# Splitting the feed-forward's normalised input into two f16 parts: on GpSimd before the transposes, instead of on ScalarE and VectorE after them

## The reference, cut to what matters

```
x = L0_attn_x                                  # (32, 256, 128) float32
x = x + 0.5 * ffn(layernorm(x))                # no gamma or beta here
x = x + attention(layernorm(x))                # 16 heads, softmax, projections, a layernorm of its own
x = x + 0.5 * ffn(layernorm(x))

def ffn(x):                                    # k0, k1, k2 are booleans: weights +1 or -1
    h = concatenate([x, -x], axis=-1)
    h = s0 * (h @ sign(k0)); h = relu(h) * 2   # 128 -> 512
    h = s1 * (h @ sign(k1)); h = relu(h) * 2   # 512 -> 512
    return s2 * (h @ sign(k2))                 # 512 -> 128
```

## Time and profile before

| | before |
|---|---|
| time, median of 3 runs | 853.59 us (852.42 to 855.54) |
| the profiled execution's own time | 853.7 us |
| its span, first to last instruction | 851.9 us |
| mean granted clock of TensorE | 0.967 |
| busy: PE, DVE, ACT, POOL | 721.5, 643.5, 513.3, 375.6 us |
| four f32 transposes of one feed-forward input (L554), 32 times | 22.2 us busy |
| its high part on ScalarE and its rest on VectorE (L1008) | 592 ns and 688 ns each |

### The profile page before, as it was taken

The page is one execution under the profiler, slowest core; times in us unless marked ns, Lnnn a source line. Parts: engine busy times, 40 slices in busy tenths (PEclk is TensorE's granted clock), DMA queues, the critical chain, the costliest instruction groups (busy, mean ns, idle before and its releaser), DMA issues. The chain is left out here.

```text
span 851.9 us, 18411 instructions
## 1 busy us (share of the span) xinstructions
PE 721.5 (85%) x7258; PEld 325.4 (38%) x7258; DVE 643.5 (76%) x1228; ACT 513.3 (60%) x739; POOL 375.6 (44%) x663
## 2 busy tenths in 40 slices
PE   6768688899998988899998888899998987977666
PEld 2433234444443434444443334344443333332333
DVE  6558778878787888878787888878787887767343
ACT  3326566766666666766666666666666666656532
POOL 4522453536355353536355453536445453435240
PEclk9989899999999999999999999999999999989797
DMA  3101010101101010101101010100101010100000
GB/s 65 38 19 45 14 45 14 58 15 40 33 4 56 15 57 15 58 14 39 33 2 58 14 58 15 57 15 32 40 3 57 14 58 3 45 15 2 15 13 12
DMA packets 29508, 25.62 MB, mean 30 GB/s; under 512 B 4336, under 2 KB 29424, under 8 KB 29424
## 3 DMA queue, kind: packets, MB, share of 16 engines
q1 hardware_dynamic: 28992, 24.07, 9.1%
q10 hardware_dynamic: 432, 0.39, 0.1%
HBM read 5.05 MB, written 4.19 MB: 11 GB/s over the span
## 5 line engine op out<-in xcount | busy, mean ns | idle before, releaser
L1055 DVE TENSOR_REDUCE row_max<-ps_s 128x4 f32<-128x1024 f32 x256 | 312.4, 1220 | 89.8 <-PE ps_s L645 89.5
L830 ACT ACTIVATE probs<-ps_t,score_scale 128x1024 f32<-128x1024 f32 x256 | 283.9, 1109 | 122.8 <-PE ps_t L658 121.3
L798 ACT ACTIVATE ffn_hi<-ps_z 128x512 f16<-128x512 f32 x288 | 168.9, 592 | 139.0 <-PE ps_z L571 76.2
L1005 DVE SCALAR_TENSOR_TENSOR ffn_lo<-ps_z,ffn_hi 128x512 f16<-128x512 f32 x256 | 174.5, 686 | 74.8 <-ACT ffn_hi L798 71.9
L570 PE MATMUL ps_z<-ffn_hi,w 128*128 128x512 f16 x512 | 196.4, 384 | 5.9 <-DVE ffn_lo L1005 5.9
L571 PE MATMUL ps_z<-ffn_lo,w 128*128 128x512 f16 x512 | 194.9, 381 | 0.0
L698 PE MATMUL ps_c<-probs,v_cols 128*32 128x256 f32 x2048 | 139.6, 391 | 0.0
L645 PE MATMUL ps_s<-k_rows,q_rows 32*128 32x256 f16 x1024 | 102.4, 278 | 39.0 <-DVE row_max L1055 31.0
L658 PE MATMUL ps_t<-q_rows,k_rows 32*128 32x256 f16 x1024 | 102.2, 278 | 4.5 <-ACT probs L830 4.5
L471 POOL TENSOR_TENSOR max_scaled<-row_max,max_unit 128x16 f32<-128x16 f32 x64 | 14.2, 222 | 176.1 <-DVE row_max L1055 176.1
L570 PEld LDWEIGHTS ps_z<-ffn_hi,w 128*128 128x128 f16 x512 | 49.9, 98 | 88.4 <-issue 24.0
(11 more groups left out here) (119 smaller groups left out, 965.0 us busy)
## 6 DMA issues: line engine op xcount, KB each, us to landing
x<-L_attn_x SPq DMA_DIRECT2D x16, 256.0 KB, 2.7
q_rows<-q_hi SPq DMA_DIRECT2D x32, 128.0 KB, 2.1
y<-x SPq DMA_DIRECT2D x16, 256.0 KB, 2.1
k_rows<-k_hi SPq DMA_DIRECT2D x30, 128.0 KB, 2.1
q_rows<-q_lo SPq DMA_DIRECT2D x16, 128.0 KB, 2.1
q_rows<-no_max SPq DMA_DIRECT2D x16, 128.0 KB, 2.1
k_rows<-k_lo SPq DMA_DIRECT2D x15, 128.0 KB, 2.1
q_rows<-max_rows SPq DMA_DIRECT2D x64, 8.0 KB
```

The source lines that it names most:

```text
L798: a_.activation(ffn_hi[:, use, :], ps_z[use % 2][:], ACT.Relu if use else ACT.Copy, scale=1.0 if use else XN_SCALE).then_inc(z_hi, 1)
L830: a_.activation(probs[grp % 2][:, j:j + 2, :], ps_t[:], ACT.Exp, scale=score_scale[:, 0:1]).then_inc(s_exp, 1)
L1005: v.scalar_tensor_tensor(out=ffn_lo[:, use, :], in0=ps_z[use % 2][:], scalar=0.0, in1=ffn_hi[:, use, :], op0=ALU.max, op1=ALU.subtract).th ...
L1055: v.tensor_reduce(row_max[hb % 2][:].rearrange("p (a l) e -> p l a e", a=2)[:, j:j + 2, :, g % 2], ps_s[:].rearrange("p l (a k) -> p l a k ...
```

## The change

GpSimd's `ffn_norm` no longer calls `normalize`. The scale of 256 goes into the power: variance plus eps is multiplied by 256 to the power -2 in the same operation (now a `tensor_scalar`). The product is then made twice, once in f32 (`ffn_xn`) and once rounded to f16 (`ffn_xh`), and a third operation subtracts the two and gives the rest in f16 (`ffn_xl`). The last one waits for both. TensorE transposes the two parts with eight f16 transposes into the same bank, read as f16. ScalarE copies the whole bank, 128 x 1024 f16, into `ffn_x` in one operation, and VectorE's part in it (L1008) is gone. The first layer waits for ScalarE's copy on a semaphore of its own, `z_in`; `z_free` counts nine for each feed-forward. The buffers `ffn_hi` and `ffn_lo` lose their number 0 and are renumbered, and SyncE's waits count by nine.

```diff
@@ ffn_norm (GpSimd)
-                normalize(ffn_xn[:], src[:], ffn_mv, ffn_xc, ffn_ve, ffn_rs, TT, f_rs, 2 * f, f_xn)
+                g.tensor_scalar(ffn_ve[:], ffn_mv[:, :, 1], EPS, XN_SCALE ** -2, ALU.add, ALU.mult).then_inc(f_rs, 1)
+                g.tensor_tensor(ffn_xc[:], src[:], ffn_mv[:, :, 0:1].broadcast_to(shape), ALU.subtract).then_inc(f_split, 1)
+                pool.wait_ge(f_rs, 2 * f + 1)
+                g.tensor_tensor(ffn_rs[:], ffn_ve[:], minus_half[:, 0:TT], ALU.pow).then_inc(f_rs, 1)
+                pool.wait_ge(f_rs, 2 * f + 2)
+                pool.wait_ge(f_split, 3 * f + 1)
+                g.tensor_tensor(ffn_xn[:], ffn_xc[:], ffn_rs[:].unsqueeze(2).broadcast_to(shape), ALU.mult).then_inc(f_split, 1)
+                g.tensor_tensor(ffn_xh[:], ffn_xc[:], ffn_rs[:].unsqueeze(2).broadcast_to(shape), ALU.mult).then_inc(f_split, 1)
+                pool.wait_ge(f_split, 3 * f + 3)
+                g.tensor_tensor(ffn_xl[:], ffn_xn[:], ffn_xh[:], ALU.subtract).then_inc(f_xn, 1)
@@ ffn_transpose, ffn_in (TensorE)
-                for i in range(TT):
-                    last = pe.transpose(bank_of(0)[:, i * P:(i + 1) * P], ffn_xn[:, i, :], ident[:])
+                for part, xx in enumerate((ffn_xh, ffn_xl)):
+                    for i in range(TT):
+                        c = part * TILE + i * P
+                        last = pe.transpose(bank_of(0)[:].bitcast(F16)[:, c:c + P], xx[:, i, :], ident16[:])
                 last.then_inc(z_full, 1)
...
-                pe.wait_ge(z_free, Z_USES * f + 1 + max(0, m - 1))
+                pe.wait_ge(z_in, f + 1)
+                at_least(pe, z_free, Z_FREES * f + max(0, m - 1))
@@ z_split (ScalarE)
-                a_.activation(ffn_hi[:, use, :], ps_z[use % 2][:], ACT.Relu if use else ACT.Copy,
-                              scale=1.0 if use else XN_SCALE).then_inc(z_hi, 1)
+                if use:
+                    a_.activation(ffn_hi[:, use - 1, :], ps_z[use % 2][:], ACT.Relu).then_inc(z_hi, 1)
+                else:
+                    a_.activation(ffn_x[:].rearrange("p c n -> p (c n)"), ps_z[0][:].bitcast(F16), ACT.Copy).then_inc(z_in, 1)
@@ z_rest (VectorE)
-                    v.scalar_tensor_tensor(out=ffn_lo[:, 0, :], in0=ps_z[0][:], scalar=XN_SCALE,
-                                           in1=ffn_hi[:, 0, :], op0=ALU.mult, op1=ALU.subtract).then_inc(z_free, 1)
```

More of the change, by code:

```diff
@@ L57 @@
 Z_USES = 10
+Z_FREES = 9
 Q_SPREADS = PARTS + 1
@@ L154, in macaron_layer @@
         ffn_xn = sb("ffn_xn", [P, TT, P])
-        ffn_hi = sb("ffn_hi", [P, 9, TILE], F16)
-        ffn_lo = sb("ffn_lo", [P, 9, TILE], F16)
+        ffn_xh = sb("ffn_xh", [P, TT, P], F16)
+        ffn_xl = sb("ffn_xl", [P, TT, P], F16)
+        ffn_x = sb("ffn_x", [P, 2, TILE], F16)
+        ffn_hi = sb("ffn_hi", [P, 8, TILE], F16)
+        ffn_lo = sb("ffn_lo", [P, 8, TILE], F16)
         att_bn = sb("att_bn", [P, TT, 6])
@@ L378, in _ @@
                 sp.dma_start(dst[:], src.partition_broadcast(P)).then_inc(s_norm_in, 16)
-            sp.wait_ge(z_free, Z_USES)
+            sp.wait_ge(z_free, Z_FREES)
             load_x(start_of(2))
@@ L550, in ffn_transpose @@
             def ffn_transpose(f):
-                at_least(pe, z_free, Z_USES * f - 1)
+                at_least(pe, z_free, Z_FREES * f - 1)
                 pe.wait_ge(f_xn, f + 1)
-                for i in range(TT):
-                    last = pe.transpose(bank_of(0)[:, i * P:(i + 1) * P], ffn_xn[:, i, :], ident[:])
+                for part, xx in enumerate((ffn_xh, ffn_xl)):
+                    for i in range(TT):
+                        c = part * TILE + i * P
+                        last = pe.transpose(bank_of(0)[:].bitcast(F16)[:, c:c + P], xx[:, i, :], ident16[:])
                 last.then_inc(z_full, 1)
             def ffn_in(f, m):
-                pe.wait_ge(z_free, Z_USES * f + 1 + max(0, m - 1))
+                pe.wait_ge(z_in, f + 1)
+                at_least(pe, z_free, Z_FREES * f + max(0, m - 1))
                 o = bank_of(1 + m)
-                pe.matmul(o[:], w0[:, m * P:(m + 1) * P], ffn_hi[:, 0, :], start=True, stop=False)
-                pe.matmul(o[:], w0[:, m * P:(m + 1) * P], ffn_lo[:, 0, :], start=False, stop=True).then_inc(z_full, 1)
+                pe.matmul(o[:], w0[:, m * P:(m + 1) * P], ffn_x[:, 0, :], start=True, stop=False)
+                pe.matmul(o[:], w0[:, m * P:(m + 1) * P], ffn_x[:, 1, :], start=False, stop=True).then_inc(z_full, 1)
             def ffn_mid(f, n):
@@ L566, in ffn_mid @@
                 o = bank_of(5 + m)
-                pe.wait_ge(z_free, Z_USES * f + max(2 + k, 4 + m))
+                pe.wait_ge(z_free, Z_FREES * f + max(1 + k, 3 + m))
                 w = w1[:, k, m * P:(m + 1) * P]
-                pe.matmul(o[:], w, ffn_hi[:, 1 + k, :], start=(k == 0), stop=False)
-                last = pe.matmul(o[:], w, ffn_lo[:, 1 + k, :], start=False, stop=(k == KC - 1))
+                pe.matmul(o[:], w, ffn_hi[:, k, :], start=(k == 0), stop=False)
+                last = pe.matmul(o[:], w, ffn_lo[:, k, :], start=False, stop=(k == KC - 1))
                 if k == KC - 1:
@@ L578, in ffn_out @@
                 if i == 0:
-                    pe.wait_ge(z_free, Z_USES * f + max(6 + k, 8))
-                pe.matmul(o, ffn_hi[:, 5 + k, i * P:(i + 1) * P], w2[:, k, :], start=(i == 0 and k == 0),
+                    pe.wait_ge(z_free, Z_FREES * f + max(5 + k, 7))
+                pe.matmul(o, ffn_hi[:, 4 + k, i * P:(i + 1) * P], w2[:, k, :], start=(i == 0 and k == 0),
                           stop=False)
-                last = pe.matmul(o, ffn_lo[:, 5 + k, i * P:(i + 1) * P], w2[:, k, :], start=False,
+                last = pe.matmul(o, ffn_lo[:, 4 + k, i * P:(i + 1) * P], w2[:, k, :], start=False,
                                  stop=(i == TT - 1 and k == KC - 1))
```

25 lines of the change are left out of this document (12 added, 13 removed).

## The result

The changed kernel takes **916.03 us** (median of 4 runs, 914.37 to 916.67), the kernel before 854.34 us beside it (4 runs). The ratio is 1.072, 95% interval 1.070 to 1.075. The forecast was 909 us in a range of 887 to 927: right in sign, mechanism and range, 7 us low. The profiled execution has a span of 914.9 us, 63.0 more than before.

What follows compares the result with a forecast made beforehand. The prediction took GpSimd's latency at step 31 to bound the kernel. Terms 30.6 (step 31) + 4 (ScalarE) + 11.4 (clock) + 6.8 (end) + 2.3 (start) = 55.1 us on 853.7 gave 909 us, range 887 to 927.

Steps and rivals of the forecast that it cites:

- What bounds the kernel: Step 31: latency of GpSimd's normalised input, not its load, is on the path; a delay there passes on one for one.
- No link with more than a few tenths of slack: Chain through one iteration, from step 31's transposes to the aggregates at the next step 27: nothing found to absorb a delay.
- GpSimd, 2.35 us: Per feed-forward on GpSimd: added product 1.04 us, subtraction 1.27 and a wait between them; bounds 2.1 and 2.9 us.
- Step 31, +30.6: Transposes of step 31, thirteen times: nothing covers GpSimd's added 2.35 us, so 13 x 2.35 = +30.6 us.
- Step 15: nothing: Step 15, thirteen times: `ffn_b`'s later input is hidden before its transposes; costed at nothing, 3 us if cover were gone.
- VectorE's predicted wait for `att_y`: Step 15: `att_y`, queued behind `ffn_b`'s input on GpSimd, makes VectorE wait 0.2 us, ahead of a 0.3 us pause.
- ScalarE, +4 (0.3 an iteration): ScalarE's longer copy delays the copy of V at step 31 by 0.1 us, `k_hi` at step 15 by 0.2; bounds 0 and 8.
- VectorE: nothing: VectorE loses 22 us of work, credited nothing because TensorE's and ScalarE's chains end later; at most 5 us in all.
- The clock, +11.4: TensorE at 1.2 GHz for some 3.3 us after most step-31 pauses: 13 x 0.8 x 1.1 us; bounds 0 and 21.
- four falls in five: Share of the thirteen step-31 pauses expected to be followed by the low clock, the 0.8 in 13 x 0.8 x 1.1.
- The end, +6.8: Two TensorE waits for maxima behind `ffn_norm`, 2 x 2.35 us, plus 2.1 us at feed-forward 31, which has nothing beside it.
- The start, +2.3: Feed-forward 0 late by 2.35 us and ScalarE's longer copy, mostly vanishing in GpSimd's pause before feed-forward 1: +2.3 us.

Runs made afterwards that it cites:

- the last experiment: Changed kernel without GpSimd's f32 product and subtraction (low part zero), VectorE's statistics of next_a one step earlier: 849.05 us, against 843.16 for the kernel before with that move.

## Why the prediction was right, and where it was off

**What bounds the kernel.** Right: latency at step 31, passed on one for one. Shown three ways: by the operations placed ahead of or behind the signal (45 us apart), by one operation (1.12 us of wait, 1.09 of interval), and by the earlier statistics. "No link with more than a few tenths of slack" held. What the account of the path lacked is the statistics themselves: they stood ahead of a rest on VectorE and held TensorE up by 0.35 us in each iteration.

**GpSimd, 2.35 us.** Measured 2.37, by two errors that cancel. The subtraction took 1.16 us, not the 1.27 of L497. And the scale in `tensor_scalar` costs: `ffn_xc` starts 0.27 us behind the start of `ffn_ve`, where it was 0.15 behind `tensor_tensor`; I had put that replacement at nothing without saying so. The estimate from the Trainium skill ("GPSIMD Engine Reference", Elementwise — side-by-side cycle accounting) for the two operations, 1.11 us each, lies between the 1.04 and 1.16 measured, and was closer on the subtraction than my row.

**Step 31, +30.6.** Measured 13 x 2.37 = 30.8. **Step 15: nothing.** Right: in an iteration that held its clock the transposes of step 15 come 24.16 us after those of step 31, before 24.08. VectorE's predicted wait for `att_y` appears (14 waits, 7.0 us in all, where before it was one of 2.2; twelve are 0.26 or 0.27, predicted 0.2) and does not reach the transposes of step 15.

**ScalarE, +4 (0.3 an iteration).** All that is downstream of GpSimd, VectorE's relief included, measured 0.21 to 0.24: the last experiment, and 50.55 - 47.97 - 2.37 in the iterations with a full clock, so some 2.8 us. The copy took 1.02 us, less than the exponentials' 1.11 that I took.

**VectorE: nothing.** Right within the tenth or two that the last experiment can't tell apart, also with GpSimd out of the way.

**The clock, +11.4.** Measured 12. I took four falls in five, and it was eleven in thirteen; 1.1 us for one, and it was 0.85 to 1.2. Here too two errors cancel: I took 1.65 us of lost work and 0.54 given back; from the transposes to the context product `ps_c` it is 3.19 us behind 450.51 and 1.76 behind 554.02, so 1.43 lost, and 0.23 given back. The sum over the twelve intervals (2.35 + 0.3 + 0.88 = 3.53 us each) gave 42.4 against the 42.0 measured.

**The end, +6.8: too small.** The part behind the last step-31 transposes grew by 13.7. The wait terms were right to a few hundredths:

```profile
812.26 0.37 PE L737 MATMUL ps_c<-ident,max_parts 128*16 128x128 f16 x2 [4.38 <-POOL max_parts L491]
855.99 0.37 PE L737 MATMUL ps_c<-ident,max_parts 128*16 128x128 f16 x2 [4.92 <-POOL max_parts L491]
893.47 0.58 PE L573 MATMUL ps_z<-ident,ffn_xh 128*128 128x128 f16 x4 [7.30 <-POOL ffn_xl L477]
```

Each is 2.37 us longer than its row of before: 2.01 and 4.93 in the earlier trace rows, and this one:

```profile
799.69 0.37 PE L717 MATMUL ps_c<-ident,max_parts 128*16 128x128 f16 x2 [2.55 <-POOL max_parts L474]
```

These are 7.1 us, and a double low stretch with ScalarE's share behind 758.62 is some 2. What I left out is the clock in the rest of the end. The segment between the last two sets of transposes (860.51 to 893.47, before 804.21 to 831.31) grew by 5.86 us for a wait that grew by 2.37, at a clock of 0.76 instead of 0.94:

```profile
860.50:893.50 33.00, 22.39 (x157) 9.59 (x154) 10.06 (x29) 10.58 (x15) 13.78 (x20) 0.76 0.03 9
```

```profile
804.20:831.30 27.10, 18.28 (x152) 8.96 (x149) 10.66 (x30) 10.16 (x15) 11.58 (x18) 0.94 0.03 11
```

The kernel with the two operations behind the signal tells what brings the low clock. It has no longer pauses at step 31, and its wait at the last transposes is as before (4.94 us); only its waits for the maxima are longer, the last one 4.85 us instead of 2.55. The same segment still takes 30.81 us instead of 27.10:

```profile
813.40:844.20 30.80, 22.55 (x152) 9.69 (x149) 10.65 (x30) 10.16 (x15) 11.74 (x19) 0.78 0.03 10
```

With one operation ahead of the signal, where that wait is 3.67 us, the clock of the segment is 0.93 and it grew by no more than its wait. All twelve kernels fall in line: where the last wait for the maxima is 2.55 to 3.67 us (six kernels) the segment's clock is 0.93 to 0.95, where it is 4.79 to 4.93 us (the other six) 0.76 to 0.83. So the low clock there comes with the longer wait for the maxima. Behind the last transposes another 0.8 us came, where I had credited 0.25.

**The start, +2.3: too small.** Up to the first step-31 transposes it is +7.3, of which 2.37 is that iteration's own, so 4.9. The transposes of feed-forwards 0 to 3 come 2.34, 3.23, 4.38 and 4.56 us later than before. So two things failed: 0.9 us of feed-forward 0's delay were left behind the pause before feed-forward 1 (3.23 less its own 2.35), and a third late input was missed. GpSimd makes feed-forward 2's directly behind the attention's input, and TensorE, which had not waited there, now does:

```profile
64.88 0.58 PE L573 MATMUL ps_z<-ident,ffn_xh 128*128 128x128 f16 x4 [1.27 <-POOL ffn_xl L477]
```

So the mechanism was right, and the two terms for the start and the end were mis-sized: 2.3 and 6.8 where 4.9 and some 12 stood. That is the 7 us between 909 and 916, less what the ScalarE term was too large. The clock at the start was not taken apart. The kernel that kept the step-31 pauses filled has the same long end (156.2 us) as the change, so the pauses at step 31 are not what makes it long.

## What to carry to other kernels

An engine that is half idle is no place for extra work if its result is waited for at once: count from the moment its input is ready to its signal, and look who stands at that signal. To move work there, first make the input ready earlier; moving VectorE's statistics and aggregates by one step was worth 32 us in the changed kernel and 12 in the old one, where taking 22 us of work from VectorE brought nothing that could be measured. Sum the start and the end with the same care as the steady part: here the added work had no cover there, and at the end the waits lengthened it twice, by themselves and through the clock.

## What the runs showed of the hardware

- The granted clock after a pause of TensorE between two busy stretches: it fell to 0.50 for about 3.4 us (6.7 around two of them) after eleven of thirteen pauses of 2.67 to 2.96 us, after ten of thirteen of 2.54 us (two operations ahead of the signal), and after the single one of 1.87 us; it held after twelve of 1.56 us and thirteen of 1.42 us. Equal pauses in equal surroundings went either way, so a share has to be estimated, not a yes or no.
- A printed idle time of TensorE is measured from the modelled end of the instruction before; from start to start the pause printed as 0.30 us cost 0.47.
- On GpSimd an f16 output costs nothing (1.041 against 1.045 us), and a subtraction of f32 and f16 operands into f16 took 1.16 us where f32 operands added into f32 took 1.27. A `tensor_scalar` on 4 elements delays the next instruction by 0.12 us more than a `tensor_tensor`.
- Eight f16 transposes and four f32 ones of 128 x 128 take the same time on TensorE, 0.45 and 0.46 us to the start of the next instruction.
